# 128-partition transfers of stored blocks, a fourth build bank, key products summed in SBUF, and a later copy of raw rows in a graph-network and feed-forward kernel

## What is computed

```python
xn = layernorm(x)
# graph network: two weighted sums over neighbours, each with a dense layer, then a projection
norm = w * rsqrt(deg_out[src] * deg_in[dst] + 1e-12)
h6 = relu(segment_sum((xn @ W6)[src] * norm, dst) + b6)
h7 = relu(segment_sum((h6 @ W7)[src] * norm, dst) + b7)
gnn = h7 @ Wp + bp
# linear attention over all nodes
k, v = head_norm(xn @ wk.T), head_norm(xn @ wv.T)      # 4 heads of 64
mix = ((xn @ wq.T) @ (k.T @ v / S)) @ wo.T + bo          # per head
x = x + gnn + mix
x = x + moe_ffn(layernorm(x))                            # two of eight experts, picked once for all rows
```

## Time and profile before

| | us |
|---|---|
| median of 3 runs (3756.12 to 3771.73) | 3768.61 |
| the profiled execution, its own time | 3737.88 |
| its span, first to last instruction | 3736.1 |
| share of the span in which PE / POOL / DVE / ACT is busy | 80% / 58% / 48% / 31% |

### The profile page before, as it was taken

The page is one execution under the profiler, slowest core; times in us unless marked ns, Lnnn a source line. Parts: engine busy times, 40 slices in busy tenths (PEclk is TensorE's granted clock), DMA queues, the critical chain, the costliest instruction groups (busy, mean ns, idle before and its releaser), DMA issues.

```text
span 3736.1 us, 52490 instructions
## 1 busy us (share of the span) xinstructions
PE 2989.6 (80%) x16152; PEld 2000.4 (54%) x16152; DVE 1794.4 (48%) x4526; ACT 1148.4 (31%) x4063; POOL 2160.5 (58%) x2090
## 2 busy tenths in 40 slices
PE   5777737888887888888874588788897888888998
PEld 4444514565555555555552356465565555655666
DVE  9888735666666666656541221422311244222334
ACT  5787734444443443434320100100100111002211
POOL 5666546676766666666765666566665666630000
PEclk8999967999999999999986799899898889998999
DMA  4331134454444544445455455455555554543221
GB/s 124 99 98 51 50 71 133 140 167 140 155 158 143 162 143 160 151 138 162 129 158 159 129 157 187 121 186 176 154 190 181 171 160 148 177 146 108 77 77 47
DMA packets 238808, 511.75 MB, mean 137 GB/s; under 512 B 61281, under 2 KB 128647, under 8 KB 232935
## 3 DMA queue, kind: packets, MB, share of 16 engines
q0 software_dynamic: 88704, 243.35, 23.0%
q1 hardware_dynamic: 143317, 258.49, 20.2%
q10 hardware_dynamic: 6500, 6.40, 0.5%
HBM read 382.96 MB, written 125.15 MB: 136 GB/s over the span
## 4 chain that ended last, share of the span: by engine, by line
PE 49%; another core or an unknown queue 11%; issue 7%; DVE 6%; ACT 3%; DMA 3%; SPq 3%; DVEq 1%; ACTq 1%; POOL 1%; POOLq 0%
PE ps L688 21%; PE ps L666 9%; PE ps L857 5%; PE ps L870 4%; PE ps L649 4%; DMA ab<-in_x 3%; SPq L2019 2%; ACT ab L1720 1%; PE ps L628 1%; PE ps L805 1%; PE ps L808 1%; DVE ab L1285 1%; DVE mlb L1252 1%; ACT mlb L1734 1%
## 5 line engine op out<-in xcount | busy, mean ns | idle before, releaser
L1943 POOL DMA_INDIRECT ringb<-t,src x1848 | 1852.9, 1003 | 982.6 <-issue 498.2
L688 PE MATMUL ps<-xb,ab 125*128 125x256 f32 (+1 forms) x4700 | 1215.0, 402 | 87.1 <-issue 72.6
L688 PEld LDWEIGHTS ps<-xb,ab 125*128 125x128 f32 x4700 | 927.1, 201 | 343.1 <-issue 181.1
L666 PE MATMUL ps<-mlb 128*125 128x300 f32 x1260 | 477.0, 471 | 171.9 <-ACT side L1724 75.6
L1720 ACT ACTIVATE ab<-ps 125x250 f32 x724 | 294.2, 406 | 730.0 <-remote 319.2
L649 PE MATMUL ps<-ringb,Sb 128*32 128x257 f32 (+1 forms) x3696 | 341.2, 421 | 134.3 <-issue 58.7
L666 PEld LDWEIGHTS ps<-mlb 128*125 128x125 f32 x1260 | 227.7, 204 | 332.5 <-issue 298.4
L1916 POOL TENSOR_TENSOR ab<-ab,wn 128x100 f32<-128x100 f32 x201 | 272.6, 1360 | 180.3 <-DVE ab L1068 180.3
L590 PE MATMUL ps<-ab 128*50 128x125 f32 x3228 | 228.3, 286 | 143.3 <-issue 55.7
L1252 DVE TENSOR_TENSOR mlb<-iof,rel 128x900 f32<-128x900 f32 (+1 forms) x231 | 232.5, 1007 | 162.0 <-remote 101.5
L590 PEld LDWEIGHTS ps<-ab 128*50 128x50 f32 x3228 | 182.3, 131 | 212.9 <-issue 122.9
(11 more groups left out here) (228 smaller groups left out, 2702.2 us busy)
## 6 DMA issues: line engine op xcount, KB each, us to landing
ad<-ab SPq DMA_DIRECT2D x42, 1562.5 KB
ab<-ad SPq DMA_DIRECT2D x210, 312.5 KB
ringb<-t,src POOLq DMA_INDIRECT x1848
kvd<-mlb SPq DMA_DIRECT2D x50, 250.0 KB
kvb<-kvd SPq DMA_DIRECT2D x50, 250.0 KB
x2t<-mlb SPq DMA_DIRECT2D x13, 500.0 KB
xb<-x2t SPq DMA_DIRECT2D x13, 500.0 KB, 8.4
xb<-in_x SPq DMA_DIRECT2D x10, 625.0 KB
```

The source lines that it names most:

```text
L666: e.matmul(PS[bank_of(t)][0:R, 0:HR], low[:, slot_of(t), :], high[:, slot_of(t), :], start=True, stop=True).then_inc(s_bld, 1)
L688: ins = e.matmul(PS[3][:, 0:wd], lhs, X[0:R, k, 0:wd], start=k == 0, stop=k == NT - 1)
L1943: e.indirect_dma_start(msg[:, slot * QT + k, 0:width], None, table, bass.IndirectOffsetOnAxis(src[:, t:t + 1], 0)).then_inc(s_g[slot], 16)
```

## The change

Four edits. (1) The stored blocks `ad` and the raw rows `kvd` get 128 rows in DRAM in place of 125, and the transfers to and from them (`store_A`, `load_A`, `kv_stored`, `kv_load`) cover all 128 partitions; DVE clears the last 32 partitions of parts of `ab` and of `raw` once at the start. (2) Builds in pass 1 use four banks (2, 7, 5, 6) in turn. (3) Bank 6 being taken, each tile's key product is made alone in bank 4, which the hidden layer also uses, and DVE adds it to a new tile `kks` (`sum_kv`) one step later; PE waits before a key product for the sum before it and for earlier hidden tiles, and before a hidden tile for earlier sums. A table `KK_AT` puts the product 0 to 2 steps after its old place, away from hidden steps. (4) In the front the raw product alternates between banks 5 and 6, and ACT copies it five batches after the tile's start instead of three. The transfers of `X`, of `X2` and of the rows after it stay at 125 partitions.

```diff
+KK_AT = {}
+for _i in range(NT):
+    _a = FIRST + KV * (_i + 1)
+    KK_AT[min(range(_a, _a + 3), key=lambda s: (sum(s + k in HID_AT for k in (-1, 0, 1)), s))] = _i
...
-        kvd = dram("kvd", [N, 2 * D])
+        kvd = dram("kvd", [NT, P, 2 * D])
-        ad = dram("ad", [DY, R, AP_])
+        ad = dram("ad", [DY, P, AP_])
+        kks = sb("kks", [P, 2 * P])
...
-            return (4, 5)[t % 2] if t >= tile_of(DY) else (2, 7, 5)[t % 3]
+            return (4, 5)[t % 2] if t >= tile_of(DY) else (2, 7, 5, 6)[t % 4]
-            return 2 if t >= tile_of(DY) else 3
+            return 2 if t >= tile_of(DY) else 4
...
-                if i >= 1:
-                    e.wait_ge(s_krc, i)
+                if i >= 2:
+                    e.wait_ge(s_krc, i - 1)
-                    ins = e.matmul(PS[5][0:R, :], xT[:, i % 2, h, :], wkv[:, h, :], start=h == 0, stop=h == 1)
+                    ins = e.matmul(PS[5 + i % 2][0:R, :], xT[:, i % 2, h, :], wkv[:, h, :], start=h == 0, stop=h == 1)
...
             def kv(s):
+                if s not in KK_AT:
+                    return
+                i = KK_AT[s]
+                e.wait_ge(s_kv, 5 * (i + 1))
+                if i >= 1:
+                    e.wait_ge(s_kka, i)
+                before = sum(1 for at in HID_AT if at < s)
+                if before:
+                    e.wait_ge(s_hadd, before)
+                for h in range(2):
+                    ins = e.matmul(PS[4][:, h * P:(h + 1) * P], kvs[0:R, D + h * P:D + (h + 1) * P],
+                                   kvs[0:R, h * P:(h + 1) * P], start=True, stop=True)
+                ins.then_inc(s_kk, 1)
...
             def hidden(i, s, slowly):
+                summed = sum(1 for at in KK_AT if at <= s)
+                if summed:
+                    e.wait_ge(s_kka, summed)
...
+            e.memset(ab[P - W:P, HOT:2 * AP_], 0.0).then_inc(s_pad, 1)
+            e.memset(raw[P - W:P, :, :], 0.0).then_inc(s_pad, 1)
...
+            def sum_kv(s):
+                if s - 1 not in KK_AT:
+                    return
+                i = KK_AT[s - 1]
+                e.wait_ge(s_kk, i + 1)
+                if i == 0:
+                    e.tensor_copy(kks[:, :], PS[4][:, 0:2 * P]).then_inc(s_kka, 1)
+                    return
+                e.wait_ge(s_kka, i)
+                e.tensor_tensor(kks[:, :], kks[:, :], PS[4][:, 0:2 * P], ALU.add).then_inc(s_kka, 1)
...
-                if c - 3 in KV_AT:
-                    kv_raw(KV_AT.index(c - 3))
+                if c - 5 in KV_AT:
+                    kv_raw(KV_AT.index(c - 5))
...
-                e.dma_start(kvd[i * R:(i + 1) * R, :], raw[0:R, k, :]).then_inc(l_kr[k], 16)
+                e.dma_start(kvd[i], raw[:, k, :]).then_inc(l_kr[k], 16)
...
-                e.dma_start(kin[0:R, k, :], kvd[i * R:(i + 1) * R, :]).then_inc(l_kx[k], 16)
+                e.dma_start(kin[:, k, :], kvd[i]).then_inc(l_kx[k], 16)
...
-                e.dma_start(ad[d][:, p * SW:(p + 1) * SW], ab[0:R, o:o + SW]).then_inc(l_as[d % 2], 16)
+                e.dma_start(ad[d][:, p * SW:(p + 1) * SW], ab[:, o:o + SW]).then_inc(l_as[d % 2], 16)
...
-                    e.dma_start(ab[0:R, q * PW:(q + 1) * PW], ad[d][:, q * PW:(q + 1) * PW]).then_inc(l_ap[p], 16)
+                    e.dma_start(ab[:, q * PW:(q + 1) * PW], ad[d][:, q * PW:(q + 1) * PW]).then_inc(l_ap[p], 16)
```

More of the change, by code:

```diff
@@ L206 @@
 X_AT = {max(at for at, m in MULT_AT[0].items() if (ND - 1, 10 * p + 9) in m) + 1: p for p in (0, 1, 3)}
-assert FIRST + KV_STEPS < STEPS0
+KK_AT = {}
+for _i in range(NT):
+    _a = FIRST + KV * (_i + 1)
+    KK_AT[min(range(_a, _a + 3), key=lambda s: (sum(s + k in HID_AT for k in (-1, 0, 1)), s))] = _i
+assert len(KK_AT) == NT and max(KK_AT) + 1 < STEPS0
 def chunk_segments(n):
@@ L425, in gnn_block @@
         PS = [ctx.enter_context(nc.psum_tensor(f"ps{i}", [P, 512], fp32)) for i in range(8)]
-        psb = {k: PS[k][0:R, 0:HR].rearrange("p (h r) -> p h r", r=RT) for k in (2, 4, 5, 7)}
+        psb = {k: PS[k][0:R, 0:HR].rearrange("p (h r) -> p h r", r=RT) for k in (2, 4, 5, 6, 7)}
         def rows_of(ap, c):
@@ L455, in gnn_block @@
         s_krc = sem("s_krc")
+        s_kka = sem("s_kka")
+        s_pad = sem("s_pad")
         s_ktr, s_kxc, s_kmm, s_kv, s_ksq, s_kk = (sem(k) for k in ("s_ktr", "s_kxc", "s_kmm", "s_kv", "s_ksq", "s_kk"))
@@ L605, in kv @@
             def kv(s):
-                n = s - FIRST
-                i, ph = divmod(n, KV)
-                if ph == 0 and 1 <= i <= NT:
-                    e.wait_ge(s_kv, 5 * i)
-                    if i == 1:
-                        e.matmul(PS[6][:, 0:2 * P], ones[0:1, :], degr[:, CR:CR + 2 * P], start=True, stop=False)
-                    for h in range(2):
-                        ins = e.matmul(PS[6][:, h * P:(h + 1) * P], kvs[0:R, D + h * P:D + (h + 1) * P],
-                                       kvs[0:R, h * P:(h + 1) * P], start=False, stop=i == NT and h == 1)
-                    ins.then_inc(s_kk, 1)
+                if s not in KK_AT:
[11 more added lines that the diff above has]
+                ins.then_inc(s_kk, 1)
             def hidden(i, s, slowly):
@@ L1366, in dve_program @@
                 for s in range(STEPS0):
+                    sum_kv(s)
                     if s - 1 in HID_AT:
@@ L1405, in dve_program @@
                 for o in (0, 64):
-                    e.tensor_scalar(bdt[o:o + 64, h, o:o + 64], PS[6][o:o + 64, h * P + o:h * P + o + 64], 1.0 / N, None,
+                    e.tensor_scalar(bdt[o:o + 64, h, o:o + 64], kks[o:o + 64, h * P + o:h * P + o + 64], 1.0 / N, None,
                                     ALU.mult).then_inc(s_bd, 1)
@@ L1633, in kv_raw @@
                 e.wait_ge(s_kmm, i + 1)
+                if i == 0:
+                    e.wait_ge(s_pad, 2)
                 if i >= 2:
                     e.wait_ge(l_kr[k], 16 * loads_of(i - 1, k))
-                e.activation(raw[0:R, k, :], PS[5][0:R, :], ACT.Copy).then_inc(s_krc, 1)
+                e.activation(raw[0:R, k, :], PS[5 + k][0:R, :], ACT.Copy).then_inc(s_krc, 1)
             for c, (t0, n) in enumerate(BATCHES):
```

4 lines of the change are left out of this document (2 added, 2 removed).

## The result

Over four runs each the changed kernel takes **3735.4 us** (3732.5 to 3742.3), the kernel before 3770.0 (3756.1 to 3771.7): ratio 0.991, 95% interval 0.989 to 0.994. The gain is 35 us where 196 were forecast; 3735 lies above the range (3455 to 3720). The profiled execution took 3732.5 us. That pair of profiles hides the gain: the one of the kernel before is 30.7 us shorter than its median, this one 2.9.

A forecast was written before the change was run, and what follows sets the result against it. The prediction took PE to bound both passes, with pass 2 idling for late block loads and `X2` rows, and DVE the front. Terms -110 - 15 - 60 + 10 - 21 = -196 from 3768.6 gave 3573 us, range 3455 to 3720.

The forecast's parts named there:

- Of the 124 us of waits named I take away 95: Pass 2: of PE's waits before dense products, gather products and turned block results, 95 us would go, bounds 0 and 124.
- Pass 2 and handoff, -125: Block transfers at 128 partitions would save 110 us in pass 2 and 15 us in the handoff.
- The loads one behind another at an estimated 2.7 us: Pass 2 caveat: a block's ten loads in sequence would take 27 us, not 13, and most of the gain would fail.
- Fourth bank, -60: Pass 1: a fourth build bank would save half of PE's 122 us of waits before builds, bounds 0 and -122.
- key sums, +10: Pass 1: adding key products on DVE would cost some 10 us through new waits of PE, bounds 0 and +150.
- The rival of the shared bank: Pass 1: each key tile stops PE twice at 3.0 us, making the kernel 88 us slower, 3857; chance 0.07.
- Front, -21: Front: the later raw copy wins DVE 25 of 35.6 us of waiting, its clears add 4; bounds +4 and -32.
- Twelve block loads in under 20 us: Sign of being right, pass 2: SP issues twelve block loads in under 20 us instead of 44.6.
- A pass 2 that stays above 1170 us with blocks landing early: Sign of being wrong: pass 2 stays above 1170 us, about 1090 being expected, although blocks land early.
- the transfers were hidden: Pass 2: idle PE time comes from DVE and ACT taking turns, earlier blocks only wait; -55, 3714; chance 0.18.
- The third, POOL as the only bound left: Both passes: only POOL's gathers, 1.25 us each, still hold them; -313 with front and handoff, 3456; chance 0.10.
- The fifth, gathers in the way: Pass 2: block loads delay gathers, 5.3 us of PE waiting per loaded block; +20, 3789; chance 0.06.

The follow-up runs named there:

- late sets: Sets of runs, each on one chip, in which the kernel before took 3740 to 3770 us; nothing about the kernels differs.
- b_again: The kernel before, unchanged, run once more for its profile: 3741.3 us (one run).
- a_again: The changed kernel, unchanged, run once more beside the kernel before: 3701.2 us, ratio 0.990.
- quick set: A set of runs on one chip in which the kernel before took 3516 or 3514 us; nothing about the kernels differs.
- b_row1: The kernel before with each load of a tenth of a block in pass 2 moving one partition instead of 125: 3371.2 us, ratio 0.959.
- a_row1b: The changed kernel with each load of a tenth of a block in pass 2 reduced to one partition, second time: 3695.1 us, ratio 0.988.
- b_wide: The kernel before with only the 128-partition transfers of blocks and raw rows and the two clears: 3382.8 us, ratio 0.962.
- b_wide2: The kernel before with the 128-partition transfers and clears alone, a second time: 3375.9 us, ratio 0.960.
- b_front: The kernel before with only the later copy of the raw product and its two banks: 3506.1 us, ratio 0.998.
- b_bank: The kernel before with only the fourth build bank and the key sums on DVE: 3522.8 us, ratio 1.002.
- wide_front: The changed kernel without the fourth bank and the key sums on DVE: 3695.9 us, ratio 0.989.
- a_plain: The changed kernel with every indirect gather replaced by a plain transfer of 128 adjacent rows: 3220.2 us, ratio 0.916.
- a_plain2: The changed kernel with plain transfers in place of all indirect gathers, a second time: 3218.4 us, ratio 0.860.
- a_mix: The changed kernel with two of the four indirect gathers of each step replaced by plain transfers: 3224.7 us, ratio 0.856.

## Why the prediction was wrong

**The step that failed** is "Of the 124 us of waits named I take away 95 ... PE idles less". It took the waits in the trace to be what paces the pass, and the largest of them, which the profile does not name, to be waits for block loads. In late sets, to which the runs of the result belong by the time of the kernel before and by their traces, PE's late signals and its standing still pace it: of the 58.9 us of "issue" before dense products the prediction took away 50, and they stayed at 59.4, 26.1 of them before and 29.6 after with PE waiting for no semaphore at all. When a transfer lands earlier, the engines that wait for PE wait for the same late signals. On one late chip, b_again and a_again, pass 2 goes from 1307 to 1283 us (-24 for -110), and pass 1 stays (1475, 1474). Loads of one partition bound the transfers from both sides. On the kernel before in a quick set they are worth 145 us (b_row1); in a late set the kernel with them, and with the other edits too, is 49 us below the kernel before (a_row1b, 3695.1 for 3744.3) and 3 below the changed one. That late signals are the link between the gathers and the time is argued from this: each run that has them is slow, and each run without them is not; no run delays signals alone.

**Pass 2 and handoff, -125.** Mechanism right: 128 partitions use all engines and the `X2` rows are in time (110.4 to 9.8 us). In quick sets also the size: b_wide -134, b_wide2 -138. By stage (b_wide against b_front for the passes and b_bank for the front, as the kernel before was not traced there) it is -143 in pass 2, -4 in the handoff, +6 in the front for the clears (+4 forecast) and +13 in pass 1, where the stores were put at 0. Those 13 us stand on POOL, whose gathers take 1.055 us each for 1.039; why is open. In late sets -24 and -4, there with the other edits in. The handoff's -15 was too much in both. The loads one behind another at an estimated 2.7 us, which the prediction held against itself, did not come: b_wide's SP issues four of them in 6.1 us. (The fixed cost of about 2 us stands on that page of the Trainium skill, DMA: Bandwidth & Descriptors, in the section Anatomy of one DMA — SWDGE (gpsimd) path, for transfers issued by GpSimd; these are issued by SP.)

**Fourth bank, -60, and key sums, +10.** Wrong in both kinds of sets. The waits before builds fell by some 95 us in the runs of the result, but they were cover: in a late set pass 1 is paced by late signals, in a quick one by POOL. Together the two edits cost 7 us in the quick set (pass 1 +15) and nothing that shows in a late one (wide_front 3695.9, all edits 3698.4). The rival of the shared bank did not come: PE waits 4.7 us in four places for sums on `kks` in pass 1 of b_bank.

**Front, -21.** 12 us with the clears (a_again) and 14 without them (b_front), of which 10 show in the time of b_front. ACT's 92.7 us did not vanish but moved to the transposed rows:

```profile
ACT mlb L1656 <- PE ps L574: 72.5, 40, 6.8
...
DVE ab L1083 <- PE ps L597: 24.0, 29, 2.3
```

DVE won 11.6 of its 35.6 us, not 25. DVE's clears cost 6 us alone and nothing beside the later copy (front 499 in b_front, 500 with them in a_row1b).

**The criteria.** "Twelve block loads in under 20 us" was a bad one: the train still took 43.3 us, because each fifth waits for PE to be done with the fifth before. It was so before the change too: of the 44.6 us of the earlier trace rows SP waited 31.3 for the semaphore that PE's dense products raise (20.6 by name, 10.7 as "remote"), and of the 43.3 us after it 35.0. The prediction read all of the 44.6 as the DMA engines holding SP; only some 13 can be that. The share of q1 was 23.2%, not above 50%. Of the rest, DVE's wait for the `X2` rows (9.8 us) and the waits before builds (50) came as forecast; PE's waits before dense products, DVE's wait for PE in the front, the 20 us of the front and both passes' lengths did not. "A pass 2 that stays above 1170 us with blocks landing early" was the sign of being wrong that appeared.

**The rivals.** The second, "the transfers were hidden", has the right outcome (3714 for 3735) by another mechanism: not DVE and ACT taking turns, but PE's signals. The third, POOL as the only bound left, is what the quick sets come to in both passes. The fifth, gathers in the way, shows in part in b_wide (71.7 us of waits for gathers for 45.3), without costing the gain. The sum of a quick set's parts, -134 - 10 + 7, gives an estimate of some 3380 us for the changed kernel; that itself was never timed there, as all three repeats fell in late sets. It would be -137 for the -196 forecast, so the two edits of pass 1 make the forecast too high even there. No kernel tried with the right sums beats the changed one by a measurable amount in a late set.

## What to carry to other kernels

A wait that the profile cannot name ("issue", "remote", "another core" in a program of one core) is a finding, not noise: compare the recorded end of the producer with the start of the waiter before costing any edit, and look whether its signals come in bunches. To learn what transfers are worth, shrink them to one row and time that, ahead of rebuilding them. And a kernel whose gathers are paced by POOL gains nothing from less PE work: look at what POOL spends on each instruction.

## What the runs showed of the hardware

- The same kernel takes 3514 to 3516 us in some sets and 3740 to 3770 in others (6.5 to 7%), at nearly equal durations of the single instructions. The distance comes with the indirect gathers on POOL and goes with them: 3218 to 3225 us in either kind with none of them (a_plain, a_plain2) and, in a late set, with half of them (a_mix).
- In the late sets PE's signals are held up, by 1.2 us in the median, 4.9 us or more for one in ten (kernel before), and come in bunches (495 of 1523 within 0.15 us of the one before, none in a quick set), while PE goes on. PE also stands still there up to 2.4 us at a time where it waits for no semaphore (64 us in the kernel before, 0 in b_front).
- Signals between engines take 0.03 to 0.05 us when prompt.
- A transfer of 125 partitions fills about five of 16 engines, one of 128 all: with 125 the traffic of pass 2 lay at 103 to 264 GB/s, with 128 bursts reach 355 to 435. In quick sets that one change is worth 3.8 to 4.0%.
- An indirect gather of 128 rows occupies POOL 0.95 to 1.09 us, with some 0.3 us until the next, a plain transfer of as many bytes 0.54 to 0.58.
